# Reordering the first mix heads, and the v branch's second linear in half-K units of 512 columns

## The reference

```
xn = layernorm(x)
x  = x + gnn(xn) + mix(xn)
x  = x + ffn(layernorm(x))

gnn(xn): q, k, v = xn @ w{q,k,v}.T + b;  q2, k2, v2 = (q, k, v) @ wi{q,k,v}.T + bi
         scores  = q2 k2.T / 8 + mask (from 6528 edges), 16 heads of 64; softmax; @ v2; @ wo.T + bo
mix(xn): q, k, v = split(xn @ Wqkv), 16 heads of 64
         spiky   = softmax over the nodes of sigmoid(relu(k @ W1 + b1) @ W2 + b2)
         scores  = q k.T / 8, scaled by spiky per node; softmax; @ v; @ Wout + bout
ffn(x):  three branches f = q, k, v, each a tree of 15 decisions that picks one of 16 leaves:
         hidden  = relu(x @ w1 + b1) of the chosen leaf (64 wide);  f(x) = hidden @ w2 + b2 of the leaf
         attention of q, k, v over the nodes, scale 1/32
```

## Time and profile before

| | |
|---|---|
| median of 3 executions | 771.73 us (771.38 to 771.84) |
| the profiled execution | 771.42 us |
| its span on the core | 769.7 us |
| TensorE busy | 748.9 us (97%) |
| VectorE busy | 474.9 us (62%) |
| ScalarE busy | 382.4 us (50%) |
| GpSimd busy | 173.3 us (23%) |

### The profile page before, as it was taken

The page is one execution under the profiler, slowest core; times in us unless marked ns, Lnnn a source line. Parts: engine busy times, 40 slices in busy tenths (PEclk is TensorE's granted clock), DMA queues, the critical chain, the costliest instruction groups (busy, mean ns, idle before and its releaser), DMA issues.

```text
span 769.7 us, 12092 instructions
## 1 busy us (share of the span) xinstructions
PE 748.9 (97%) x4754; PEld 721.0 (94%) x4754; DVE 474.9 (62%) x943; ACT 382.4 (50%) x658; POOL 173.3 (23%) x139
## 2 busy tenths in 40 slices
PE   4998999999999999999999999999999999999998
PEld 3988999999999999999999999889999999999997
DVE  6878766774776677766666665666654444451542
ACT  5544556654655665686868554234443334331530
POOL 4724232322422230251212755300000000000000
PEclk9999999999999999999999999999999999999999
DMA  5511332232133223213131613323333333221302
GB/s 200 195 56 56 110 110 73 93 110 108 59 108 110 78 88 141 110 56 110 56 111 55 247 56 131 110 110 110 110 110 109 126 146 112 110 110 54 111 1 82
DMA packets 14389, 79.59 MB, mean 103 GB/s; under 512 B 3216, under 2 KB 3504, under 8 KB 5616
## 3 DMA queue, kind: packets, MB, share of 16 engines
q1 hardware_dynamic: 11088, 74.45, 26.8%
q0 software_dynamic: 2960, 4.26, 1.7%
q10 hardware_dynamic: 288, 0.14, 0.1%
HBM read 76.66 MB, written 2.19 MB: 102 GB/s over the span
## 4 chain that ended last, share of the span: by engine, by line
PE 87%; DVE 7%; ACT 3%; issue 1%; DMA 0%; DVEq 0%; ACTq 0%
PE g_bank L1431 47%; PE g_bank L1456 16%; PE o_bank L1512 4%; PE t_bank L1501 4%; PE s_bank L1813 2%; PE s_bank L1489 2%; PE s_bank L1490 2%; PE s_bank L1385 2%; PE g_bank L1385 2%; PE t_bank L1813 1%; DVE w_lo L873 1%; PE t_bank L1797 1%; ACT q_st L531 1%; DVE junk L1028 1%; PE o_bank L1543 1%
## 5 line engine op out<-in xcount | busy, mean ns | idle before, releaser
L1431 PE MATMUL g_bank<-act_hi,w_hi 128*128 128x384 f32 x616 | 214.7, 349 | 0.8 <-DVE k_st L915 0.8
L1431 PE MATMUL g_bank<-act_hi,w_lo 128*128 128x384 f32 x616 | 206.7, 335 | 0.0
L1431 PE MATMUL g_bank<-act_lo,w_hi 128*128 128x384 f32 x616 | 206.2, 335 | 0.0
L873 DVE TENSOR_TENSOR w_lo<-raw,w_hi 128x2048 fp32r<-128x2048 f32 x59 | 138.4, 2345 | 32.9 <-ACT w_hi L496 32.2
L496 ACT ACTIVATE w_hi<-raw 128x2048 fp32r<-128x2048 f32 x67 | 127.9, 1909 | 27.4 <-PE s_bank L1813 12.5
L1431 PEld LDWEIGHTS g_bank<-act_hi,w_hi 128*128 128x128 f32 x616 | 116.0, 188 | 3.9 <-issue 3.7
L1431 PEld LDWEIGHTS g_bank<-act_lo,w_hi 128*128 128x128 f32 x616 | 116.0, 188 | 0.0
L1431 PEld LDWEIGHTS g_bank<-act_hi,w_lo 128*128 128x128 f32 x616 | 115.6, 188 | 0.0
L416 POOL DMA_INDIRECT edge_table<-ew,eidx x51 | 66.7, 1308 | 156.6 <-DMA edge_table<-ew,eidx 155.8
L1016 DVE TENSOR_TENSOR pT_lo<-t_bank,pT_hi 128x384 fp32r<-128x384 f32 x96 | 50.6, 553 | 33.5 <-ACT pT_hi L597 33.0
L597 ACT ACTIVATE pT_hi<-t_bank 128x384 fp32r<-128x384 f32 x96 | 43.7, 489 | 43.0 <-PE t_bank L1501 42.7
(11 more groups left out here) (269 smaller groups left out, 1550.5 us busy)
## 6 DMA issues: line engine op xcount, KB each, us to landing
raw<-wstream_dram SPq DMA_DIRECT2D x68, 1024.0 KB, 4.8
x_sb<-x_dram SPq DMA_DIRECT2D x3, 512.0 KB, 4.8
y_acc<-x_dram POOLq DMA_DIRECT2D x3, 512.0 KB, 5.7
out_dram<-out_sb SPq DMA_DIRECT2D x6, 256.0 KB, 2.0
edge_table<-ew,eidx POOLq DMA_INDIRECT x51, 2.2
edge_table<-mask POOLq DMA_DIRECT2D x1, 576.0 KB, 3.6
mask<-edge_table POOLq DMA_DIRECT2D x1, 576.0 KB, 8.1
bo_b<-bo_dram POOLq DMA_DIRECT2D x1, 512.0 KB, 7.2
```

The lines of the kernel that those rows point to most:

```text
L873: V.tensor_tensor(flat(w_lo[s][:, :, :]), raw[:, s, :], flat(w_hi[s][:, :, :]), ALU.subtract) \
L1431: last = mm(out, w2[a], x2[b], start=k == 0 and a + b == 0, stop=not after and k == KT - 1 and a == 1)
```

## The change

- GpSimd does the subtraction of one unit more, `mix_v(0) + 1` (VectorE did it), and begins that of `mix_v(0)` only when `row_v` reads 2, which is when VectorE's first `row_third` has ended.
- VectorE's and ScalarE's order in the opening four units: `take_K(0)` goes ahead of the softplus steps, key tiles 6 to 9 move forward on both TensorE and VectorE, and three instead of four key tiles are left for the V unit. With gi = 0, ScalarE does the first `exps` before `take_V(0)` and VectorE does `maxima` before it.
- The first `head_scores` goes from behind the V unit's first half into it (tile 1, after its seventh k), and the first head's transposes and the second head's scores move forward by one step of k.
- In groups 1 to 3, `exp_row` and `row_third` go ahead of the drain of Q's first half (`take_Q(n + 5, 0)`).
- The v branch's second linear becomes `v2_unit`: units of 512 columns by half of K. For a column half c the three node tiles lie in three banks (`v_bank`) while both K halves are added, then the bias (512 columns wide). Its weights are cut by `halves`. `split_hi` of the units behind it waits for `v_half` or for all of column half 0.

The diff, cut: the layout of `b2_st` (one tensor [P, 2, MB] in place of two), `last_bias` over 512 columns, the names of the banks and the host's `halves` for the v branch are left out, and `gemm_N` loses the hooks that only the old tail used.

```diff
@@ -67,7 +68,7 @@
...
-ON_POOL = (U_A0, mix_v(0), U_GNN + 4, U_GNN + 5, U_GNN + 7, U_GNN + 8, U_GNN + 10, U_GNN + 11, U_OUT + 1)
+ON_POOL = (U_A0, mix_v(0), mix_v(0) + 1, U_GNN + 4, U_GNN + 5, U_GNN + 7, U_GNN + 8, U_GNN + 10, U_GNN + 11, U_OUT + 1)
@@ -406,7 +411,9 @@
...
                 own.done(nc.gpsimd.tensor_tensor(ew[:, :], ew[:, :], code, ALU.add))
+            pool.wait_ge(row_v, 2)
             split_lo(mix_v(0))
+            split_lo(mix_v(0) + 1)
             pool.wait_ge(key_free, KEY_TILES)
@@ -491,6 +498,10 @@
...
+                elif n.it is None and n.base == U_V2 + 2:
+                    act.wait_ge(v_half, 1)
+                elif n.it is None and n.base == U_V2 + 3:
+                    act.wait_ge(g_full, V_FILL0 + NT)
@@ -650,10 +660,10 @@
...
+            take_K(Index(U_K0), 0, None)
...
-            for m in range(2):
-                take_K(Index(U_K0), m, None)
+            take_K(Index(U_K0), 1, None)
@@ -672,10 +682,14 @@
...
-                take_pT(tile, (0, 1))
-                if h < HG - 1:
+                if (g.base, h) == (0, 0):
+                    take_pT(tile)
...
-                take_pT(tile, (2,))
+                else:
+                    take_pT(tile, (0, 1))
+                    if h < HG - 1:
+                        exps("mix", g, h + 1, (0,))
+                    take_pT(tile, (2,))
@@ -693,8 +707,9 @@
...
+                    exps("mix", g, 0, (0,))
...
-                    exps("mix", g, 0)
+                    exps("mix", g, 0, (1, 2))
@@ -719,8 +734,8 @@
...
                     tanh_row(g + 1)
+                    exp_row(g + 1)
                     take_Q(n + 5, 0, None)
-                    exp_row(g + 1)
                     take_alpha(g + 1)
@@ -835,27 +851,22 @@
...
-            for u in range(GROUPS):
-                n = Index(UNITS - GROUPS + u)
-                cols = slice(u * MB, (u + 1) * MB)
-                if u < GROUPS - 1:
-                    split_hi(n + 1)
-                for half in range(2):
-                    take_N(n, half, vf_hi, cols)
-                if u < GROUPS - 1:
-                    last_bias(u + 1)
-                if u == 0:
-                    for t in range(NT):
-                        q = S_FFN0 + t
-                        act.wait_ge(e_in, q + 1)
-                        nc.scalar.activation(pf_ring[:, t, :], s_bank[q % 3][:, 0:N], ACT.Exp, bias=nbias[:, t:t + 1],
-                                             scale=FFN_SCALE, accum_out=esum[:, t:t + 1]).then_inc(e_done, 1)
-                if u == 1:
-                    for t in range(NT):
-                        act.wait_ge(t_full, T_FFN0 + t + 1)
-                        nc.scalar.activation(pTf_hi[:, :, t * P:(t + 1) * P],
-                                             t_bank[t % 2][:, 0:N].rearrange("p (m n) -> p m n", n=P),
-                                             ACT.Copy).then_inc(t_hi, 1)
+            split_hi(Index(U_V2 + 1))
+            for t in range(NT):
+                q = S_FFN0 + t
+                act.wait_ge(e_in, q + 1)
+                nc.scalar.activation(pf_ring[:, t, :], s_bank[q % 3][:, 0:N], ACT.Exp, bias=nbias[:, t:t + 1],
+                                     scale=FFN_SCALE, accum_out=esum[:, t:t + 1]).then_inc(e_done, 1)
+            split_hi(Index(U_V2 + 2))
+            take_v2(0)
+            for t in range(NT):
+                act.wait_ge(t_full, T_FFN0 + t + 1)
+                nc.scalar.activation(pTf_hi[:, :, t * P:(t + 1) * P],
+                                     t_bank[t % 2][:, 0:N].rearrange("p (m n) -> p m n", n=P),
+                                     ACT.Copy).then_inc(t_hi, 1)
+            last_bias(1)
+            split_hi(Index(U_V2 + 3))
+            take_v2(1)
@@ -894,11 +905,13 @@
...
-            def take_N(n, half, hi, lo, cols):
-                g_hi_wait(fill_of(n) + half)
-                t0, nt = (0, 2) if half == 0 else (2, 1)
-                V.tensor_tensor(lo[:, t0:t0 + nt, cols], g_bank[half][:, 0:nt * MB].rearrange("p (t m) -> p t m", m=MB),
-                                hi[:, t0:t0 + nt, cols], ALU.subtract).then_inc(g_free, 1)
+            def take_v2(c):
+                for t in range(NT):
+                    g_hi_wait(Index(V_FILL0 + NT * c + t))
+                    at = slice(c * 512, (c + 1) * 512)
+                    V.tensor_tensor(vf_lo[:, t, at], v_bank[c][t][:, :], vf_hi[:, t, at], ALU.subtract) \
+                     .then_inc(g_free, 1)
@@ -1082,18 +1095,18 @@
...
+            take_K(Index(U_K0), 0, None)
+            key_tile(1)
...
-            key_tile(1)
+            dve.wait_ge(w1_ready, 1)
+            V.tensor_tensor(w1_lo[:, :], w1_raw[:, :], w1_hi[:, :], ALU.subtract).then_inc(w1_ready, 1)
...
-            dve.wait_ge(w1_ready, 1)
-            V.tensor_tensor(w1_lo[:, :], w1_raw[:, :], w1_hi[:, :], ALU.subtract).then_inc(w1_ready, 1)
-            take_K(Index(U_K0), 0, None)
+            take_K(Index(U_K0), 1, None)
...
-            take_K(Index(U_K0), 1, None)
@@ -1101,14 +1114,15 @@
...
+            key_tile(6)
...
-            key_tile(6)
...
+            key_tile(8)
...
-            key_tile(8)
+            key_tile(9)
...
-            for c in range(9, KEY_TILES):
+            for c in range(10, KEY_TILES):
@@ -1118,11 +1132,11 @@
...
-                    split_lo(n + 1)
+                    maxima("mix", g, 0)
...
-                    maxima("mix", g, 0)
+                    normals("mix", g, 0, (0, 1))
...
-                    normals("mix", g, 0)
+                    normals("mix", g, 0, (2,))
@@ -1163,8 +1177,8 @@
...
+                    row_third(g + 1)
...
-                    row_third(g + 1)
@@ -1342,35 +1358,29 @@
...
-            for u in range(GROUPS):
-                n = Index(UNITS - GROUPS + u)
-                cols = slice(u * MB, (u + 1) * MB)
-                if u < GROUPS - 1:
-                    split_lo(n + 1)
-                for half in range(2):
-                    take_N(n, half, vf_hi, vf_lo, cols)
-                if u < GROUPS - 1:
-                    last_bias(u + 1)
-                if u == 0:
-                    for t in range(NT):
-                        q = S_FFN0 + t
-                        dve.wait_ge(s_full, q + 1)
-                        own.done(V.reduce_max(nbias[:, t:t + 1], s_bank[q % 3][:, 0:N], AX_X))
-                        V.tensor_scalar(nbias[:, t:t + 1], nbias[:, t:t + 1], -FFN_SCALE, None, ALU.mult) \
-                         .then_inc(e_in, 1)
-                    for t in range(NT):
-                        normalise(pf_ring, Index(S_FFN0 + t), t)
-                if u == 1:
-                    for t in range(NT):
-                        dve.wait_ge(t_hi, hi_turn(T_FFN0 + t) + 1)
-                        at = slice(t * P, (t + 1) * P)
-                        V.tensor_tensor(pTf_lo[:, :, at], t_bank[t % 2][:, 0:N].rearrange("p (m n) -> p m n", n=P),
-                                        pTf_hi[:, :, at], ALU.subtract).then_inc(t_free, 1)
+            split_lo(Index(U_V2 + 1))
+            for t in range(NT):
+                q = S_FFN0 + t
+                dve.wait_ge(s_full, q + 1)
+                own.done(V.reduce_max(nbias[:, t:t + 1], s_bank[q % 3][:, 0:N], AX_X))
+                V.tensor_scalar(nbias[:, t:t + 1], nbias[:, t:t + 1], -FFN_SCALE, None, ALU.mult) \
+                 .then_inc(e_in, 1)
+            for t in range(NT):
+                normalise(pf_ring, Index(S_FFN0 + t), t)
+            split_lo(Index(U_V2 + 2))
+            take_v2(0)
+            for t in range(NT):
+                dve.wait_ge(t_hi, hi_turn(T_FFN0 + t) + 1)
+                at = slice(t * P, (t + 1) * P)
+                V.tensor_tensor(pTf_lo[:, :, at], t_bank[t % 2][:, 0:N].rearrange("p (m n) -> p m n", n=P),
+                                pTf_hi[:, :, at], ALU.subtract).then_inc(t_free, 1)
+            last_bias(1)
+            split_lo(Index(U_V2 + 3))
+            take_v2(1)
...
-                dve.wait_ge(g_full, fill_of(Index(UNITS)).value() + i + 1)
+                dve.wait_ge(g_full, OUT_FILL0 + i + 1)
@@ -1584,14 +1588,17 @@
...
-                if (m, k) in ((0, 2), (0, 7), (1, 4)):
-                    key_tiles(6 + ((0, 2), (0, 7), (1, 4)).index((m, k)))
+                if (m, k) in ((0, 0), (0, 4), (1, 0), (1, 5)):
+                    key_tiles(6 + ((0, 0), (0, 4), (1, 0), (1, 5)).index((m, k)))
...
-                if (t, k) in ((0, 1), (0, 5), (1, 1), (1, 5)):
-                    key_tiles(9 + ((0, 1), (0, 5), (1, 1), (1, 5)).index((t, k)))
+                if (t, k) in ((0, 1), (0, 5), (1, 1)):
+                    key_tiles(10 + ((0, 1), (0, 5), (1, 1)).index((t, k)))
+                if (t, k) == (1, 6):
+                    pe.wait_ge(key_free, KEY_TILES)
+                    head_scores("mix", first, 0)
@@ -1610,8 +1617,6 @@
...
-                    pe.wait_ge(key_free, KEY_TILES)
-                    head_scores("mix", g, 0)
@@ -1619,11 +1624,12 @@
...
```

(85 more changed lines are left out.)

34 lines of the change are left out of this document (19 added, 15 removed).

## The result

The changed kernel takes 765.48 us (median of 4, 765.13 to 765.65) against 771.67 (771.38 to 771.84): 0.9919 of the time before, 95% interval 0.9906 to 0.9931. That is 6.2 us less, 1.0 above the 764.5 predicted and inside 763.5 to 767.0. The profiled execution's span is 763.7 us (before 769.7).

The account below looks back on a forecast made before the run. TensorE, busy 748.9 of 769.7 us, was taken as the bound. Opening 4.1, groups 1.2 and tail 2.0 sum to 7.3 off 771.42: 764.1, median 764.4, plus 0.1 for places without cover: 764.5 us, 8-in-10 range 763.5 to 767.0.

Parts of the forecast that it names:

- The gaps of the opening: Five TensorE waits between 27 and 73 us, 4.50 us in sum; 4.1 to be won, bounds 1.9 and 4.5.
- gap 3: Opening, first scores waiting for the last key tile: 0.86 us lost, 0.5 to be won, about 0.35 to stay.
- Gap 2: Opening, `weights_T` waiting for `row_third`, held beside GpSimd's subtraction: 0.90 us, to go entirely.
- gaps 1 and 5: Opening: second unit's first fill waiting for `take_K(0)`, 0.95 us, and first `head_out` waiting for `pT_lo`, 0.54; both to go.
- The cover at the V unit: First transposes: GpSimd holds the first maxima product until 59.9; transposes and TensorE both near 63.5, hardly any cover.
- Rival B: First V unit keeps its wait, costing 1 to 2.3 us; 5.0 to 6.3 won, time 766.1; chance 0.22.
- The groups: Groups 1 to 3, wait before `weights_T` goes: 3 x 0.39 = 1.2 us, bounds 0 and 1.2.
- The tail: Second linear of the v branch: 144 matmuls of 512 columns replace 288 of 256; 36.0 to 34.0 us, 2.0 won.
- gap 1: Opening, second unit's first fill waiting for VectorE's `take_K(0)` behind the softplus step: 0.95 us, to go entirely.

Follow-up runs that it names:

- the tail alone: The kernel before with only `v2_unit`, `take_v2` and the `halves` layout new, all of the rest old: 769.93 us against 771.90 beside it.

## Why the prediction was nearly right

**The gaps of the opening.** Forecast 4.1, found 4.49 from F on: all but gap 3 closed, and that was left with 0.38 from start to start against the 0.35 forecast. Two sizes were off and nearly hide each other. Gap 2 was 0.82 and not 0.90, since `weights_T` follows its neighbour by 1.08 before and by 0.26 now. Against it, instructions behind a gap also run longer: the first six transposes take 0.82 now and 1.07 in the earlier trace rows, and the first matmul behind gaps 1 and 5 costs 0.25 in place of 0.17. With 0.4 for these the sum is 4.5. The first scores started at 59.19, which is 58.1 less the late start of 1.1.

**The cover at the V unit.** The maxima product was held until GpSimd ended (61.00 against 60.98), as the prediction took it. The Trainium skill ("SBUF — State Buffer", section "SBUF: two separate sides") has an exclusive lock for two SBUF inputs; the trace agrees, down to an instruction of one column. Rival B did not occur: the normalised tiles ended at 64.06 and TensorE came at 64.62. That cover is due to the order (the other 1.1 of the 1.79) more than to the split (0.7), which I had not separated.

**The groups.** The step "0.56 - 0.17 = 0.39 us" was mis-sized, and with it the 1.2 of the sum. `weights_T` follows a 384-column matmul by 0.27 where it does not wait, not by 0.17, so a gap is 0.28 and three make 0.84, not 1.17; the run with the old order gave 0.8.

**The tail.** 2.0 forecast, 2.10 in the profile, 2.08 and 1.76 (by width alone) in the two runs that isolate it. The split of the last unit ended at 738.87, for a unit whose first matmul came at 739.0: no wait, by 0.1 to 0.2, as forecast:
```profile
736.58 2.29 DVE L884 TENSOR_TENSOR w_lo<-raw,w_hi 128x2048 fp32r<-128x2048 f32 x1 [1.04 <-ACT w_hi L507]
```

**What the sum lacked.** From F to the end the gain is 734.24 - 727.18 = 7.06 us by the means of two profiles each, against a sum of 7.3 less 0.1; it contains the 0.35 lost at 340 us, which no step foresaw. The median shows 6.2. The likely reason is one that a single profile could not show: gap 1's 0.95 was counted in an execution with an early F, 19.85 against 20.33 in the kernel's second profile. At F of 20.8 to 21.0, as in both profiles of the changed one, the old gap would have cost 0.3 to 0.5 (0.28 + 0.16 in the tail alone), which leaves 6.5; the last 0.3 is within the spread of the medians. That the executions without a profile had an F like the profiled ones is assumed, not shown. The sum took a gap that other delays run into for one of fixed length. That the total came out within 1.0 owes something to errors in both directions: more than forecast in the opening, less in the groups, at 340 us and in gap 1.

## What to carry to other kernels

A small VectorE instruction that works on SBUF alone costs, beside a long GpSimd one, what is left of the latter; those with an operand in PSUM were not held (in the changed kernel a comparison at 45.12, inside GpSimd's subtraction, took its usual 0.34). So move the long one behind a known end of the small ones, and look where a small one lands whenever it is moved. Price a gap against the start-to-start distance of the same pair of instructions where they do not wait. A gap early in a program takes up whatever makes the start vary: read several executions before counting it in full, and compare kernels from a point behind the start.

## What was not expected of the hardware

- TensorE's first matmuls run near half rate (0.336 us for 384 columns, later 0.174) while the granted clock is printed as 1.00; the moment of full rate differs between executions enough to move F from 20.3 to 21.6 with the same kind of opening. Dummy work kept it at full rate, and gave nothing, since VectorE's split at 18.7 to 21.0 is next.
- VectorE stops for nearly half a us (0.37 beyond the usual distance) in front of one instruction, and with one instruction added the stop is seen 313 us later. At the head it cost 0.35 us, in the ffn nothing.
- A VectorE step of four columns took 4.55 us beside GpSimd's subtraction, one of a single column 1.04 (alone 0.17 and 0.16).
